# Seven split down blocks a tile instead of five, their low parts on two engines

## What is computed

```python
x = x + layernorm(attention(layernorm(x)))           # 16 heads of 8
x = x + layernorm(ffn(layernorm(x)))

# ffn, for T = 4096 tokens
scores = sigmoid(x @ gate_w.T)                        # 32 experts
# the 4 best of 8 groups by the sum of their two best scores + bias, then the 6 best experts
topk_w = 2.5 * picked / (picked.sum() + 1e-20)
h = relu(einsum('th,eih->tei', x, up_w)) ** 2         # 64 wide for each expert
moe = einsum('tei,ehi->th', h * combine, down_w)
out = moe + relu(x @ shared_up_w.T) ** 2 @ shared_down_w.T
```

## Time and profile before

| | us |
|---|---|
| median of 3 runs | 500.38 |
| lowest, highest | 499.31, 500.88 |
| the profiled execution's own time | 500.0 |
| span of that execution's profile | 498.2 |
| TensorE busy | 467.0 |
| VectorE busy | 387.9 |
| ScalarE busy | 356.0 |
| GpSimd busy | 248.5 |

### The profile page before, as it was taken

The page is one execution under the profiler, slowest core; times in us unless marked ns, Lnnn a source line. Parts: engine busy times, 40 slices in busy tenths (PEclk is TensorE's granted clock), DMA queues, the critical chain, the costliest instruction groups (busy, mean ns, idle before and its releaser), DMA issues.

```text
span 498.2 us, 10729 instructions
## 1 busy us (share of the span) xinstructions
PE 467.0 (94%) x3365; PEld 269.9 (54%) x3366; DVE 387.9 (78%) x1001; ACT 356.0 (71%) x707; POOL 248.5 (50%) x593
## 2 busy tenths in 40 slices
PE   6598999999999999998999899999999999999994
PEld 3233454554444445553456566666666666666662
DVE  4787888889899999889748788695968869496453
ACT  3415888888888878877676686868698776866551
POOL 7453233335666745427132627658393764626251
PEclk9777999999999999999899999999999999999999
DMA  8444444444444454420044254565453546445421
GB/s 234 145 120 156 131 126 115 136 140 136 138 135 145 133 151 141 137 67 3 3 171 132 80 186 137 165 185 176 115 206 95 165 148 191 175 121 202 132 102 42
DMA packets 49049, 67.48 MB, mean 135 GB/s; under 512 B 3808, under 2 KB 35808, under 8 KB 48992
## 3 DMA queue, kind: packets, MB, share of 16 engines
q1 hardware_dynamic: 48992, 66.78, 43.0%
HBM read 51.17 MB, written 15.20 MB: 133 GB/s over the span
## 4 chain that ended last, share of the span: by engine, by line
PE 72%; DVE 13%; issue 7%; DMA 3%; ACT 2%; POOL 1%; SPq 1%; POOLq 0%; DVEq 0%; ACTq 0%
PE pO L1330 9%; PE pY L1411 8%; PE pS L1411 8%; DVE mneg L986 8%; PE pS L1272 7%; PE pS L1395 6%; PE pS L1397 6%; PE pS L1396 6%; PE pS L1278 3%; DMA qk<-qk_scratch 2%; PE pY L1359 2%; PE pX L1257 2%; PE pY L1347 1%; PE pS L1442 1%; PE pX L1375 1%
## 5 line engine op out<-in xcount | busy, mean ns | idle before, releaser
L986 DVE TENSOR_REDUCE mneg<-pS 128x2 f32<-128x512 f32 x256 | 161.8, 684 | 23.9 <-PE pS L1272 21.5
L770 ACT ACTIVATE probs<-pS 128x512 f32<-128x512 f32 x256 | 141.3, 596 | 40.4 <-PE pS L1278 39.1
L1272 PE MATMUL pS<-qk 48*128 48x256 bf16 x512 | 87.9, 282 | 13.2 <-DMA qk<-qk_scratch 3.6
L855 ACT ACTIVATE h_ring<-r 128x512 f32<-128x512 f32 x104 | 64.3, 624 | 34.7 <-DVE r L1117 26.4
L1395 PE MATMUL pS<-qk,up_hi 128*128 128x512 f32 x144 | 88.4, 614 | 0.0
L1278 PE MATMUL pS<-qk 51*128 51x256 bf16 x512 | 85.3, 277 | 0.3 <-ACT probs L770 0.3
L1330 PE MATMUL pO<-probs,vv 128*32 128x256 f32 x1024 | 73.4, 395 | 0.0
L1272 PEld LDWEIGHTS pS<-qk 48*128 48x128 bf16 x512 | 34.4, 96 | 67.0 <-DVE mneg L986 35.2
L1117 DVE SCALAR_TENSOR_TENSOR r<-pS,probs 128x512 f32<-128x512 f32 x64 | 43.6, 689 | 27.3 <-PE pS L1397 26.4
L1397 PE MATMUL pS<-qk,up_lo 128*128 128x512 f32 x144 | 57.0, 396 | 0.0
L1396 PE MATMUL pS<-qk,up_hi 128*128 128x512 f32 x144 | 56.8, 394 | 0.0
(11 more groups left out here) (201 smaller groups left out, 830.3 us busy)
## 6 DMA issues: line engine op xcount, KB each, us to landing
c_ring<-c_scratch SPq DMA_DIRECT2D x32, 512.0 KB, 4.1
probs<-c_scratch SPq DMA_DIRECT2D x32, 512.0 KB, 4.1
qk<-qk_scratch SPq DMA_DIRECT2D x64, 192.0 KB
qk_scratch<-q_parts SPq DMA_DIRECT2D x16, 192.0 KB, 2.3
qk_scratch<-k_parts SPq DMA_DIRECT2D x16, 192.0 KB, 2.4
qk_scratch<-q_parts SPq DMA_DIRECT2D x16, 128.0 KB, 2.7
qk_scratch<-k_parts SPq DMA_DIRECT2D x16, 128.0 KB, 2.5
out_x<-probs SPq DMA_DIRECT2D x7, 256.0 KB, 4.6
```

What stands on the lines that cost most here:

```text
L770: nc.scalar.activation(probs[j][:, hh], s2_bank(n)[:, :, :], ACT.Exp, scale=SCALE).then_inc(exp_done, 1)
L855: nc.scalar.activation(h_ring[:, (n - at) % HRING], r_sb[n % URING][:, :], ACT.Square).then_inc(sq_done, 1)
L986: nc.vector.tensor_reduce(mneg[u % 2][:, :, hh, k], pS1[n % S1_RING][:, :].rearrange("p (a s) -> p a s", a=TH), AX.X, ALU.max, negate=True ...
L1272: return mm(pS1[n % S1_RING][:, T * th:T * (th + 1)], qp[slot][rows, k, P * th:P * (th + 1)], kp[slot][rows, k, :], start=True, stop=True)
```

## The change

Blocks 2, 4, 6, 8, 10, 12 and 14 of each tile are split, seven in place of five. GpSimd makes the low parts of the first four, VectorE those of the last three (`low_h`, in steps 13, 15 and 16, into two buffers of its own in a part of qk that the attention has left). h_hi and h_whole have four buffers instead of three. ScalarE no longer waits for the low part before it overwrites h_whole. The high and low parts of the down weights, which GpSimd makes once during the attention, hold 7 x 128 columns instead of 5 x 128.

```diff
-SPLIT = (2, 5, 8, 11, 14)
-SPLIT_LAG, HI_RING, LO_RING = 6, 3, 2
+SPLIT = (2, 4, 6, 8, 10, 12, 14)
+SPLIT_LAG, HI_RING, LO_RING = 6, 4, 2
+
+LOW_AT = {13: 4, 15: 5, 16: 6}
+OWN = 4
...
+        PER = (OWN, len(SPLIT) - OWN)
+
+        def low_user(own, turn):
+
+            i, s = divmod(turn, PER[own])
+            return len(SPLIT) * i + s + OWN * own + 1
...
                 low(i, 0)
                 if i + 2 < NTILE:
                     residual1(i + 2)
+                low(i, 1)
                 if i == 0:
-                    low(i, 1)
                     low(i, 2)
                 if i + 1 < NTILE:
                     root_of_sum(i + 1)
                 if i >= 1:
-                    low(i, 1)
+                    low(i, 2)
                 if i + 2 < NTILE:
                     chain_x1(i + 2)
-                if i >= 1:
-                    low(i, 2)
+                low(i, 3)
                 if i >= 1:
                     chain_f(i - 1)
-                low(i, 3)
-                low(i, 4)
...
-                    if at >= HI_RING:
-                        act.wait_ge(lo_done, at - HI_RING + 1)
-                    elif at == 1:
+                    if at == 1:
                         act.wait_ge(pv_done, 4 * NB)
...
+            def low_h(i, s):
+                n = FBLK * i + SPLIT[s]
+                at, turn = splits_to(n), PER[1] * i + s - OWN
+                dve.wait_ge(hi_done, at + 1)
+                dve.wait_ge(sq_done, n + 1)
+                if turn >= len(h_lo2):
+                    dve.wait_ge(split_done, low_user(1, turn - len(h_lo2)))
+                nc.vector.tensor_tensor(h_lo2[turn % len(h_lo2)], h_whole[at % HI_RING], h_hi[at % HI_RING].bitcast(F32),
+                                        ALU.subtract).then_inc(lo2_done, 1)
...
+                    if k in LOW_AT:
+                        low_h(i, LOW_AT[k])
...
-                pe.wait_ge(lo_done, at + 1)
-                high, low = h_hi[at % HI_RING], h_lo[at % LO_RING]
+                own = int(s >= OWN)
+                turn = PER[own] * i + s - OWN * own
+                pe.wait_ge((lo_done, lo2_done)[own], turn + 1)
+                high, low = h_hi[at % HI_RING], (h_lo, h_lo2)[own][turn % LO_RING]
```

More of the change, by code:

```diff
@@ L202, in block_kernel @@
         spare = probs[4][:, :, :, :].rearrange("p a b c -> p (a b c)")
-        h_whole = [h_ring[:, HRING], spare[:, 0:TILE], spare[:, TILE:2 * TILE]]
-        h_hi, h_lo = ([sb(f"{name}{i}", [P, TILE], F32R)[:, :] for i in range(n)]
-                      for name, n in (("h_hi", HI_RING), ("h_lo", LO_RING)))
+        spare2 = probs[5][:, :, :, :].rearrange("p a b c -> p (a b c)")
+        h_whole = [h_ring[:, HRING], spare[:, 0:TILE], spare[:, TILE:2 * TILE], spare2[:, 0:TILE]]
+        unit_tail = [qk[slot][:, half:half + UB // 2].rearrange("p j a b -> p (j a b)").bitcast(F32R)
+                     for slot, half in ((4, 0), (4, UB // 2), (5, 0))]
+        h_hi = [sb(f"h_hi{i}", [P, TILE], F32R)[:, :] for i in range(HI_RING - 1)] + unit_tail[0:1]
+        h_lo = [sb(f"h_lo{i}", [P, TILE], F32R)[:, :] for i in range(LO_RING)]
+        h_lo2 = unit_tail[1:3]
         down_hi, down_lo = (sb(f"down_{n}", [P, len(SPLIT), D], F32R) for n in ("hi", "lo"))
-        down_whole = down_sb[:, :, :].rearrange("p (a b) d -> p a b d", b=3)[:, 0:len(SPLIT), 0]
+        down_whole = down_sb[:, :, :].rearrange("p (a b) d -> p a b d", b=2)[:, 0:len(SPLIT), 0]
         fT_sb = sb("fT_sb", [P, TILE])
-        assert all(k - SBLK == 3 * s for s, k in enumerate(SPLIT))
+        assert all(k - SBLK == 2 * s for s, k in enumerate(SPLIT))
         assert (HRING + 1) * TILE == RBLK * P and TILE >= SI
@@ L303, in block_kernel @@
         sq_done = sem("sq_done")
-        hi_done, lo_done = sem("hi_done"), sem("lo_done")
+        hi_done, lo_done, lo2_done = sem("hi_done"), sem("lo_done"), sem("lo2_done")
         split_done = sem("split_done")
@@ L639, in low @@
                 n = FBLK * i + SPLIT[s]
-                at = splits_to(n)
+                at, turn = splits_to(n), PER[0] * i + s
                 pool.wait_ge(hi_done, at + 1)
                 pool.wait_ge(sq_done, n + 1)
-                if at >= LO_RING:
-                    pool.wait_ge(split_done, at - LO_RING + 1)
-                nc.gpsimd.tensor_tensor(h_lo[at % LO_RING], h_whole[at % HI_RING], h_hi[at % HI_RING].bitcast(F32),
+                if turn >= LO_RING:
+                    pool.wait_ge(split_done, low_user(0, turn - LO_RING))
+                nc.gpsimd.tensor_tensor(h_lo[turn % LO_RING], h_whole[at % HI_RING], h_hi[at % HI_RING].bitcast(F32),
                                         ALU.subtract).then_inc(lo_done, 1)
```

## The result

The changed kernel takes 505.0 us (median of 4 runs, 503.22 to 505.68) against 499.85 us (median of 4 runs of before, 498.81 to 500.88): ratio 1.0099, 95% interval 1.0077 to 1.0121: 1.0% slower, clear of the noise. The profiled execution took 505.38 us with a span of 503.6 us. 505.8 was forecast, from a base of 500.0.

A forecast was written before the change was run, and what follows sets the result against it. TensorE's streaming bounds the feed-forward stage while VectorE's rectified blocks and ScalarE's squares arrive in time. 500.0 - 2.6 saved + 6.1 waits in tiles 1 to 5 + 2.3 first tile = 505.8 us; range 499.8 to 507.2.

The forecast's parts named there:

- The direction and the place: Slower; TensorE waits about one us at block 7's plain down in tiles 1 to 5, released by ScalarE's square.
- The step that the forecast turned on: VectorE's root_c after comb: waits out GpSimd's next pass, ending 1.4 us later, or is served right after comb.
- root_c finds the pass running: Tiles 1 to 5: root_c waits out block 4's low part, ending 1.4 us later; 505.8 us, chance 0.52.
- root_c slips through: Rival: root_c served right after comb, tiles 1 to 5 wait 0.13 us each; 500.4 us, chance 0.23.
- Tiles 1 to 5: TensorE waits 0.97 us at block 7's down, 0.26 more at block 9's: 1.23 a tile, 6.1 us in all.
- The reason given for the late chain: Split of block 12 in step 0 starts VectorE's routing 0.6 us later; root_c also waits out a GpSimd pass.
- The saving: TensorE: each block changed to split saves 0.16 us, two per tile in eight tiles, 2.6 us.
- The first tile: Tile 0: TensorE waits, including 1.8 us for block 8's low part, add 2.3 us net, bounds 1.4 and 3.0.
- the gain: First tile: comb no longer beside a GpSimd pass, so the chain is 0.5 to 1.0 us earlier; 0.75 subtracted.
- Tile 6: Tile 6, with no residual add, was to be 0.3 us shorter, as was tile 7.
- VectorE's low parts: Three subtractions a tile in steps 13, 15 and 16, 2.0 us of work, covered and costing nothing.
- The sum: Feed-forward terms: saving 2.6, tiles 1 to 5 plus 6.1, first tile plus 2.3; from 500.0 to 505.8 us.

The follow-up runs named there:

- first experiment: Changed kernel with GpSimd's low part of block 4 ahead of the residual add in tiles 1 to 7; 499.11 us, ratio 0.9971.
- second experiment: Kernel before (five splits) with the low part of block 5 moved directly behind the residual add; 503.32 us, ratio 1.0068.

## Why the prediction was right

**The direction and the place** were right: the wait stands at block 7's down in tiles 1 to 5, the square ends it, and root_c takes 1.47 us where 1.4 more than 0.38 was forecast. The first experiment takes it away by nothing but the order on GpSimd, the second makes it by nothing but that order.

**The step that the forecast turned on** was the choice between "root_c finds the pass running" (505.8) and "root_c slips through" (500.4), by the second pass of the earlier trace rows being stretched by only 0.05 us. After, the second pass takes 1.33 us to the first one's 1.29: VectorE's operation is let in between two passes for one operation, comb, and the next one waits out the second pass whole. The Trainium skill (SBUF — State Buffer, section "SBUF: two separate sides") calls the shared ports an exclusive lock for the whole instruction; the rows of root_c agree, at 1.47 us beside a pass of 1.33.

**Tiles 1 to 5**: 1.23 us of waiting a tile forecast. The tiles take 29.98 us, and TensorE's own work is 28.74 (29.06 less twice 0.16), so 1.24 us. Of this 0.27 stand between the downs of blocks 7 and 9, and 0.97 at block 7's: the row says 0.71 idle, but the down starts 1.10 us after the last matmul of the up block (362.31 to 363.41), where it would start 0.23 after, and its own pair takes 0.57 us instead of 0.46. Rect of block 7 stands 1.38 us later in the tile than before; 1.4 was forecast.

**The reason given for the late chain** was half right. Its first operation begins at 350.12, 4.19 us into the tile (before 3.60), 0.6 later as forecast, because of the split in step 0. But what counts is up block 4, and the split need not stand in step 0 for that. As a second cause beside the port I had given it too much: alone it costs no wait at block 7's down (first experiment). It only eats lead, so that the same order on GpSimd costs 1.1 us a tile and not 0.78 (second experiment).

**The saving**: in the kernel with the order mended a tile takes 28.88 to 28.92 us against 29.06, some 0.16 less; 0.32 was forecast for no wait at all, and 0.34 less (28.23 against 28.57) is what the one tile without any wait shows.

**The first tile**: +2.3 us was the term beside the saving. TensorE has 1.0 us less down work inside this tile: 0.3 is saved, and the 0.70 of block 12's split falls in the next. So the tile should have grown by 1.3 us; it grew by 0.9, so the term was 1.9, inside its bounds. The waits for block 9's square and block 8's low part are 1.49 and 1.55 us; the second was forecast at 1.8. Timeline after, which answers the earlier trace rows:

```profile
269.45 2.53 POOL L659 TENSOR_TENSOR h_lo<-probs,h_hi 128x512 fp32r<-128x512 f32 x2
...
272.83 0.29 DVE L1089 SCALAR_TENSOR_TENSOR comb<-e_left,score 128x128 f32<-128x128 f32 x1
...
274.86 1.13 PE L1432 MATMUL pS<-h_ring,down_sb 128*128 128x512 f32 x2 [1.49 <-ACT h_ring L864]
...
279.29 1.26 POOL L659 TENSOR_TENSOR h_lo<-probs,qk 128x512 fp32r<-128x512 f32 x1
280.61 0.50 PE L1444 MATMUL pS<-qk,down_hi 128*128 128x512 f32 x1 [1.55 <-POOL h_lo L659]
```

comb is clear of the passes and takes 0.29 us, where it took 1.34. It begins 0.34 us later in the tile than before, so it ends 0.7 us earlier, and the down of block 9 starts 0.7 us earlier too (27.96 us into the tile, before 28.67): the gain was taken at 0.75.

**Tile 6** was wrong: 0.3 us shorter forecast, 0.4 longer found. The step that failed is that only the neighbour of the residual add was looked at. In tile 6, which has none, the low part of block 4 starts as soon as its whole is there, and that is beside masked, an operation of two SBUF inputs in the middle of the chain (1.27 us). The term was left out; it is 0.7 us. Tile 7 with the end isn't 0.3 us shorter either but 0.4 longer; that is no wait, since by this way of measuring it begins with the 0.70 of block 12's split from the tile before.

**VectorE's low parts** at no cost: right. They take 0.70 us, no one waits for them, and 16.5 us more of them cost 1.3 to 2.3.

**The sum** for the feed-forward stage was 5.8 us, and 6.0 were found. That it is so close is in part luck: the first tile's 0.4 us too much and the five tiles' 0.2 too much (before's tile 4 was 0.3 long) stand against the 0.7 us that was missing in tile 6. The median difference is 5.15, and 5.8 at equal clock; the rest is the attention at another clock.

## What to carry to other kernels

Before a pass that holds the shared port is moved on one engine, look at which operation of the other engine's critical chain, a small copy included, will stand beside it, and at what is next in line behind that pass: two passes in a row cover 2.5 us of the chain, and which of them comes first decided over 1.1 us a tile here. In these runs the early low part was cheap where it lay beside no operation of the chain that it could hold up. A gain of 0.16 us a block is lost to one collision of 1.1 us a tile, and a chain with several short operations offers the next victim when one is freed.

## What the runs showed of the hardware

- An operation of VectorE in line while two GpSimd passes follow each other is let in between them (comb, 0.48 us, ended 0.14 us behind the first), and the second pass is stretched by only 0.04 us (1.33 against 1.29). The next VectorE operation with two SBUF inputs then takes the whole second pass: 1.47 us against 0.38.
- When VectorE's operation meets a GpSimd pass the start decides, within 0.1 us: masked took 0.28 us when it began 0.03 us ahead of the pass and 1.34 when it began 0.09 behind. The pass ahead of which it had slipped took 1.40 us for 1.29.
- Copies with one input of 128x24 elements wait as well: 0.99, 1.10 and 1.30 us beside a pass, 0.18 elsewhere. I had counted operations with two inputs only. The Trainium skill (the same page and section) names VectorE's two-port modes beside two-input operations, and says that a float32 copy within SBUF runs in such a mode; these rows agree.
- The other way round, a GpSimd operation on 128x4 elements takes 0.78 us for 0.20 beside a VectorE subtraction of 128x512, though its own row begins 0.03 us ahead of it.
- The time of this kernel between executions goes with the mean granted clock, 2.7 us for each 0.01, which is over half a per cent. A difference of 0.3% between two kernels can be made of it. Most of it lies in the attention, but the feed-forward stage isn't free of it: in one execution a wait of 2.10 us was followed by a clock of 0.50 and 1.5 us more, in another by neither.
